# A graph kernel's edge stage: TensorE issues each step's second gate products ahead of the second pair's sums and the one-hots' transposes

## What is computed

```
q, k, v = x_norm @ Wq.T + bq, x_norm @ Wk.T + bk, x_norm @ Wv.T + bv      # per node, 256 wide
dk = silu(edge_attr @ Wdk.T + bdk);  dv = silu(edge_attr @ Wdv.T + bdv)   # per edge, 64 -> 256
attn = silu(sum(q[dst] * k[src] * dk)) * cosine_cutoff(edge_weight)       # one number per edge
msg  = v[src] * dv * attn
agg  = segment_sum(msg, dst);  x = layernorm(x + x + agg @ Wo.T + bo)
```

## Time and profile before

| | us |
|---|---|
| median of three runs | 2602.67 |
| the profiled execution | 2599.69 |
| its span, first to last instruction | 2598.1 |
| PE busy in the span | 2343.7 |
| DVE busy in the span | 2220.7 |
| ACT busy in the span | 1920.7 |
| POOL busy in the span | 1723.3 |

### The profile page before, as it was taken

The page is one execution under the profiler, slowest core; times in us unless marked ns, Lnnn a source line. Parts: engine busy times, 40 slices in busy tenths (PEclk is TensorE's granted clock), DMA queues, the critical chain, the costliest instruction groups (busy, mean ns, idle before and its releaser), DMA issues. The chain is left out here.

```text
span 2598.1 us, 52015 instructions
## 1 busy us (share of the span) xinstructions
PE 2343.7 (90%) x12456; PEld 1874.5 (72%) x12456; DVE 2220.7 (85%) x6384; ACT 1920.7 (74%) x4081; POOL 1723.3 (66%) x1818
## 2 busy tenths in 40 slices
PE   5469969999999999999999999999999999999976
PEld 4335537777778777877778777777877877787764
DVE  5376639999999999999999999999999999999965
ACT  1257627877888888888888887888888878888844
POOL 3455017777777777777777777777777777777723
PEclk8779989999999999999999999999999999999987
DMA  8777439999999999999999999999999999999943
GB/s 269 207 176 201 157 119 270 273 273 269 276 271 280 280 275 279 276 273 277 272 277 277 275 275 274 274 277 280 275 279 273 277 272 277 270 282 281 274 138 115
DMA packets 318252, 662.30 MB, mean 255 GB/s; under 512 B 79334, under 2 KB 131666, under 8 KB 318224
## 3 DMA queue, kind: packets, MB, share of 16 engines
q0 software_dynamic: 137824, 446.91, 58.8%
q1 hardware_dynamic: 172272, 205.20, 26.6%
q10 hardware_dynamic: 8128, 9.90, 1.2%
HBM read 602.50 MB, written 59.30 MB: 255 GB/s over the span
## 5 line engine op out<-in xcount | busy, mean ns | idle before, releaser
L979 POOL DMA_INDIRECT e_kv<-kv_tab,e_idx x1604 | 1565.7, 976 | 551.5 <-issue 481.7
L1097 ACT ACTIVATE e_gate_ps<-e_gate_ps 128x1024 f32<-128x1024 f32 x802 | 810.1, 1010 | 381.4 <-PE e_gate_ps L1030 381.4
L1159 DVE TENSOR_TENSOR e_gated<-e_kv,e_gate_ps 128x1024 f32<-128x1024 f32 x804 | 973.7, 1211 | 90.0 <-DMA e_kv<-kv_tab,e_idx 47.4
L1017 PE MATMUL e_sum_ps<-e_gated,e_weighed_hot 128*128 128x256 f32 x3232 | 829.2, 379 | 23.8 <-issue 21.5
L1029 PE MATMUL e_gate_ps<-wd_hi_lo,e_high 128*128 128x512 f32 x1604 | 730.3, 455 | 35.3 <-DVE e_gated L1159 33.4
L1017 PEld LDWEIGHTS e_sum_ps<-e_gated,e_weighed_hot 128*128 128x128 f32 x3232 | 582.3, 189 | 104.4 <-issue 22.3
L1169 DVE CUSTOM_DVE_ANT_0 e_gated<-e_gated,e_q_ps 128x256 f32<-128x256 f32 x1608 | 603.3, 409 | 55.9 <-PE e_q_ps L1049 54.1
L1030 PE MATMUL e_gate_ps<-wd_bias,e_low 128*128 128x512 f32 x1604 | 632.9, 395 | 0.0
L1107 ACT ACTIVATE e_weighed_hot<-e_hot,e_attn 128x128 f32<-128x128 bf16 x1612 | 525.5, 398 | 15.4 <-DVE e_attn L1179 5.8
L1048 PE MATMUL e_q_ps<-e_q_win,e_hot_t 128*128 128x256 f32 x1604 | 406.2, 286 | 66.2 <-issue 65.6
L1029 PEld LDWEIGHTS e_gate_ps<-wd_hi_lo,e_high 128*128 128x128 f32 x1604 | 302.1, 188 | 138.9 <-issue 75.3
(11 more groups left out here) (149 smaller groups left out, 1513.3 us busy)
## 6 DMA issues: line engine op xcount, KB each, us to landing
e_attr<-attr_groups_dram SPq DMA_DIRECT2D x800, 128.0 KB
e_kv<-kv_tab,e_idx POOLq DMA_INDIRECT x1604
e_q_win<-q_tab SPq DMA_DIRECT2D x100, 256.0 KB
sum_tab<-e_sums SPq DMA_DIRECT2D x102, 128.0 KB
e_prior<-sum_tab SPq DMA_DIRECT2D x101, 128.0 KB
q_tab<-l_q_out SPq DMA_DIRECT2D x50, 256.0 KB, 2.6
kv_tab<-l_kv_out SPq DMA_DIRECT2D x50, 256.0 KB, 3.0
xt_tab<-xt_out SPq DMA_DIRECT2D x50, 132.0 KB, 2.8
```

The source lines that it names most:

```text
L979: pool.indirect_dma_start(kv[:, k, :], None, kv_tab, bass.IndirectOffsetOnAxis(ap=idx[:, k:k + 1], axis=0)).then_inc(kv_landed[k // G][k % ...
L1017: last = nc.tensor.matmul(sum_ps[:, 0:H], weighed_hot[:, c % 2, k, :], gated[:, c * G + k, H:2 * H], start=(c == 0 and k == 0), stop=(c == ...
L1097: nc.scalar.activation(gate_ps[:, 2 * p:2 * p + 2, :], gate_ps[:, 2 * p:2 * p + 2, :], ACT.Silu).then_inc(silu_ready[s][p], 1)
L1159: nc.vector.tensor_tensor(gated[:, pair(s, p), :], kv[:, pair(s, p), :], gate_ps[:, 2 * p:2 * p + 2, :], ALU.mult).then_inc(gated_ready[s] ...
```

## The change

In each of the four steps TensorE issues `gates(c, 1)` right behind `gates(c, 0)`, and then `segment_sum(c, 1)` and `turn_hot(c)`. No instruction, wait or semaphore is added or removed, and the other engines' programs are as they were.

```diff
                     for c in range(GROUPS):
                         segment_sum(c, 0)
                         gates(c, 0)
+                        gates(c, 1)
                         segment_sum(c, 1)
                         turn_hot(c)
-                        gates(c, 1)
                         of = visit.of
```

## The result

The changed kernel took 2925.37 us (median of four runs, 2921.32 to 2925.92) against 2603.91 for the kernel before; the ratio is 1.123, 95% interval 1.120 to 1.125. The forecast was 2886 in a range from 2780 to 2950: the right way, by 283 us where 321 came, so it is 39 us short. One profiled execution of it took 2924.0 us of span.

A forecast was written before the change was run, and what follows sets the result against it. Four resources stood close together in the edge stage's 21.00 us visit, PE at 19.2; the new order makes a loop the bound. 7.56 + 3 x 5.34 + 0.25 = 23.83 us per visit, 283 us more: 2886 us, range 2780 to 2950.

The forecast's parts named there:

- The loop: Ordinary steps: dot_rows, gate_rows(c, 1), gates(c, 1), sums, transposes and gather_q close a loop of 5.34 us, above PE's 4.81.
- take_sums and the turn of DVE's loop: Step 3 to step 0: take_sums waits for the later segment_sum(3, 1), the loop's turn counts in full; 7.56 us.
- The window of q: Step 1's products wait for the window's load, issued when step 0's products end; 0.25 us per visit, bounds 0 and 0.55.
- Hidden chains: Transposes, copy_hot, silu(c, 1), next gate_rows: 5.07 to 5.5 us beside the loop, likely hidden; at most 45 us in all.
- POOL's slack gives nothing: POOL and gathers get 3 us of slack per visit, DVE's waits for k and v vanish; no gain.
- Softer ends: Rival: the loop's turn is hidden and the window of q lands in time; 188 us more, 2791 us; chance 0.17.
- Only a part binds: Rival: DVE runs far enough ahead that only take_sums costs, 1.3 us per visit, some 2730 us; chance 0.08.
- Faster: Rival: second gate products start at once and PE's waits go, with POOL stopping the gain at 2552 us; chance 0.03.
- The clock: Rival: PE's idle pieces drop its clock in the edge stage, 3290 us; chance 0.06, shared with other losses above 2945.

The follow-up runs named there:

- f2: Kernel before with the new order in steps 0 to 2 alone, step 3 keeping the old one: 2775.21 us, ratio 1.066.
- f1: Kernel before with the new order in step 3 alone, steps 0 to 2 keeping the old one: 2740.43 us, ratio 1.053.
- e6: Changed kernel with DVE taking take_sums behind dot_rows(3, 1) instead of ahead of it: 2907.56 us, ratio 1.119.
- e7: Changed kernel with the window of q loaded once ahead of the loop, and no load or wait per visit: 2866.61 us, ratio 1.104.
- e5: Changed kernel with each call of dot_rows waiting for its own pair of gather_q alone: 2861.64 us, ratio 1.101.
- e12: Changed kernel with dot_rows waiting pair by pair, take_sums behind dot_rows(3, 1), and the window of q in a second buffer that ScalarE copies: 2841.89 us, ratio 1.095.
- e1: New order in step 3 alone, measured earlier, when the kernel before took 3674.97 us: 3876.28 us, ratio 1.056.
- e4: Order gates(c, 0), turn_hot(c), gates(c, 1), segment_sum(c, 1), measured when the kernel before took 3674.97 us: 3730.86 us, ratio 1.015.
- f3: Kernel before with gates(c, 1) moved behind segment_sum(c, 1) but still ahead of turn_hot(c), against the kernel before: 2618.85 us, ratio 1.007.
- e3: Kernel before with gates(c, 1) taken only past turn_hot(c), measured earlier, when the kernel before took 3674.97 us: 3801.49 us, ratio 1.036.

## Why the prediction was right, and where it was short

- *The loop.* Right, link by link. The forecast had 5.34 and 5.39 came. The 0.05 is in gather_q: behind the transposes it takes 1.34 us from its start to the first dot product (1210.81 to 1212.15), where I had 1.27. Three stretches of 0.05 make 15 us. f2 has the loop without the term of step 3, 5.39 in both plain stretches.
- *take_sums and the turn of DVE's loop.* Right: 7.56 against 7.53, and f1 shows it alone, 1.55 us of stretch. To take the turn in full was right as well: e6 shows that the wait for the sums doesn't hide it.
- *The window of q.* The mechanism was right and the size was off: I took 0.25 of a possible 0.55 because DMA would have more air. It has (0.83 instead of 0.93), but step 1's products come no sooner: they start 4.76 us behind the end of step 0's in the mean, 4.64 in the kernel before, and 4.20 where nothing is loaded (e7). So it is 0.55. That is 30 us, the largest part of the 39. With the 15 of the loop and 3 back from take_sums the terms come to 42, so the number isn't right by errors that cancel.
- *Hidden chains.* Right: silu(c, 1) behind copy_hot stays under the loop, by 0.19 (e5).
- *POOL's slack gives nothing.* Right: 419 us of waits for indices, and DVE's waits for k and v gone.
- *The rivals.* "Softer ends" fell with e6 and e7. "Only a part binds" fell with f2: steps 0 to 2 alone cost 170 us. "Faster" fell with the result. The clock stayed at 1.00 in the changed kernel but for 3.4 us of the first visit. The Trainium skill ("TensorE: Matmul & The Clock Gate", the section on the second HAM failure mode) tells of a kernel in which frequent short idle times between groups of matmuls made the clock swing between its two levels. The changed kernel's trace doesn't show that, with pieces of 0.54, 0.33 and 1.09 us in each visit; e12's does, in 39 visits of 98.

What stays open: why the window's load comes no sooner at 0.83 of DMA than at 0.93, what decides in which visit of e12 the clock falls, what made the time of e1 to e4 slow, and what the order of e4 is worth.

## What to carry to other kernels

When an instruction that waits is moved ahead of work that doesn't, ask what that work had covered, and add up the loop that closes through the other engines: a cover taken away (here 1.06 us of sums and transposes) shows in every turn of the loop once it is longer than the slack (0.53 here), even where the engine had time to spare; the 0.19 of the transposes alone showed only where the path ran through them already (f3). Then look for what waits for the work that was put back, here take_sums, once per visit and nearly half of the loss. Where a loop runs close beside another, a cure of one gains only the distance to the next.

## What the runs showed of the hardware

A turn of DVE's outer loop is 1.45 us of register operations and a load in DVE's sequencer. It costs 0.61 us of idleness where 0.68 us of work (two dot products) stand between take_sums and the turn, and 1.04 us where none does (e6). The wait ahead of take_sums, 0.91 us in e6, hides nothing of it. With two idle pieces of PE of about 0.9 and 1.1 us close behind each other, its clock fell in 39 of 98 visits of e12 and in 7 of 98 of e6; with 0.54, 0.33 and 1.09 it didn't (the changed kernel). In e3, when the kernel before took 3674.97 us, what waited for PE's transposes started 2.27 us behind them in the mean instead of 0.04, and what waited for gather_q 2.51 us instead of 0.15, while the packets of the gathers took 0.22 us as ever.
